# A two-layer transformer kernel on one core: other slots for the same work, the output product in two parts, the setup inside the first slots

## The reference, cut to what matters

```python
xn = layernorm(x)                                   # x: [16, 512, 128]
x  = x + attn0(xn) + ffn0(xn)
xn = layernorm(x)
x  = x + attn1(xn) + moe(xn)

attn0: 16 heads of 8; rope; bias within 64 keys; causal softmax;
       elastic = relu(probs + tau[h] / (row + 1)); (elastic @ v) @ Wo.T
ffn0:  fp4(silu(fp4(xn) @ fp4(Wg).T) * (fp4(xn) @ fp4(Wu).T)) @ fp4(Wd).T    # 352 wide, blocks of 16
attn1: rope; q, k = elu(q) + 1, elu(k) + 1; causal linear attention; @ w_out
moe:   4 experts, the best 2 of a softmax, and a shared one; 344 wide
```

## Time and profile before

| | |
|---|---|
| time, median of 3 runs (lowest to highest) | 2467.56 us (2466.31 to 2469.77) |
| the profiled execution's own time | 2475.17 us |
| its span | 2473.3 us |
| mean granted TensorE clock | 0.939 |
| first scores of round 0; of round 1 | 50.0 us; 151.8 us |
| rounds 2 to 14, each | 148.1 to 151.4 us |
| last round's start to the end | 234.3 us |
| busy: PE, DVE, ACT, POOL | 88%, 74%, 51%, 47% |

### The profile page before, as it was taken

One profiled execution on the slowest core, in us unless ns is written; L12 is line 12 of the kernel. 1 busy time (PEld: TensorE's weight loads), 2 busy tenths in 40 slices (PEclk: granted clock), 3 DMA queues, 4 the chain that ended last, 5 costly groups with the idle time before them and its releaser, 6 DMA issues.

```text
span 2473.3 us, 52472 instructions
## 1 busy us (share of the span) xinstructions
PE 2178.1 (88%) x18761; PEld 1395.3 (56%) x18761; DVE 1820.4 (74%) x5695; ACT 1258.1 (51%) x3477; POOL 1155.4 (47%) x1809
## 2 busy tenths in 40 slices
PE   3788989889898898989889898898989989898988
PEld 2454655646465564655646565565655656565555
DVE  5667868678786877878678686877778678786755
ACT  1555555554544545555554545545455554545532
POOL 6574454534545364454534545354454544534320
PEclk8779989989999999989999899998999989999999
DMA  3000000000000000000000000000000000000000
GB/s 112 5 6 1 1 14 2 14 1 10 5 2 14 1 15 1 1 14 2 14 1 10 5 2 14 1 14 1 2 14 2 14 1 1 10 2 10 2 9 5
DMA packets 33542, 22.03 MB, mean 9 GB/s; under 512 B 2443, under 2 KB 32771, under 8 KB 33283
## 3 DMA queue, kind: packets, MB, share of 16 engines
q1 hardware_dynamic: 33283, 18.68, 2.6%
HBM read 14.48 MB, written 4.19 MB: 8 GB/s over the span
## 4 chain that ended last, share of the span: by engine, by line
PE 69%; DVE 17%; issue 7%; POOL 4%; ACT 3%; DVEq 0%; ACTq 0%; POOLq 0%
PE ps L1084 10%; PE ps L1157 9%; PE ps L1164 8%; PE ps L1216 7%; PE ps L1098 5%; PE ps L1074 4%; DVE ring L491 3%; PE ps L1053 3%; PE ps L1201 3%; PE ps L1150 3%; PE ps L1191 2%; PE ps L1143 2%; PE ps L1062 2%; PE ps L1180 2%; PE ps L1151 2%
## 5 line engine op out<-in xcount | busy, mean ns | idle before, releaser
L801 POOL TENSOR_SCALAR ring<-ring,row_rcp,tau_row 128x128 f32<-128x128 f32 (+3 forms) x1024 | 621.3, 613 | 920.9 <-DVE row_rcp L498 920.6
L903 ACT ACTIVATE ring<-ring,neg_max 128x128 f32<-128x128 f32 (+3 forms) x1024 | 569.1, 556 | 528.8 <-DVE neg_max L491 528.8
L1084 PE MATMUL ps<-identf,ring 128*128 128x128 f32 x2560 | 405.9, 298 | 14.9 <-ACT qkT L894 5.8
L491 DVE CUSTOM_DVE_ANT_1 ring<-ps,bias_t 128x384 f32<-128x384 f32 (+1 forms) x496 | 288.9, 618 | 159.1 <-PE ps L1074 157.0
L1084 PEld LDWEIGHTS ps<-identf,ring 128*128 128x128 f32 x2560 | 295.2, 149 | 86.7 <-issue 23.0
L1216 PEld LDWEIGHTS ps<-ed_t,h 128*128 128x128 f32 (+1 forms) x1920 | 250.6, 191 | 80.6 <-issue 77.6
L1157 PE MATMUL ps<-xn1T,eg_t 128*128 128x512 f32 (+1 forms) x480 | 275.2, 656 | 9.8 <-DVE h L567 9.5
L491 DVE CUSTOM_DVE_ANT_0 ring<-ps,bias_t 128x128 f32<-128x128 f32 (+1 forms) x528 | 170.7, 359 | 139.5 <-PE ps L1074 139.2
L1216 PE MATMUL ps<-ed_t,h 128*128 128x128 f32 (+1 forms) x1920 | 272.7, 278 | 0.0
L1164 PE MATMUL ps<-xn1T,eu_t 128*128 128x512 f32 (+1 forms) x480 | 258.4, 620 | 8.3 <-DVE h L576 5.8
L937 ACT ACTIVATE tanh<-ps 128x512 f32<-128x512 f32 (+1 forms) x240 | 141.3, 589 | 235.9 <-PE ps L1157 235.6
(11 more groups left out here) (154 smaller groups left out, 3378.3 us busy)
## 6 DMA issues: line engine op xcount, KB each, us to landing
x_t<-x SPq DMA_DIRECT2D x16, 256.0 KB, 2.8
x<-x SPq DMA_DIRECT2D x16, 256.0 KB, 2.9
out<-x SPq DMA_DIRECT2D x16, 256.0 KB, 2.3
bias_t<-bias SPq DMA_DIRECT2D x1, 1536.0 KB
eg_t<-eg SPq DMA_DIRECT2D x1, 860.0 KB
eu_t<-eu SPq DMA_DIRECT2D x1, 860.0 KB
ed_t<-ed SPq DMA_DIRECT2D x2, 320.0 KB
ring<-inv_row SPq DMA_DIRECT2D x1, 256.0 KB, 2.6
```

What stands on the lines that cost most here:

```text
L491: dve.tensor_tensor_reduce(out=dst, in0=src, in1=add, scale=-1.0, scalar=NO_MIN, op0=ALU.add, op1=ALU.min, accum_out=neg_max[:, n % 2, r:r ...
L801: pool.tensor_scalar(e, e, row_rcp[:, m % 2, r:r + 1], tau_row[:, i, HG * g + r:HG * g + r + 1], ALU.mult, ALU.add).then_inc(p_ok.sem, 1)
L903: act.activation(e, e, ACT.Exp, bias=neg_max[:, n % 2, r:r + 1], scale=-1.0, accum_out=row_sum[:, n % 2, r:r + 1]).then_inc(exp_ok.sem, 1)
L1084: last = pe.transpose(o[:, r * P:(r + 1) * P], ring_of(i, r)[:, k * P:(k + 1) * P], idf)
```

## The change

The order of the work changes; of the arithmetic, only the order of the summands of the output product and the engines that do the FP4 of the weights. Places by slot (p before, then after):

- gate and up products of layer 0: 14, 15, 16, 17; now 12, 14, 16, 18. Maxima follow by 2, the step moves from 24 to 21, rounding constants from 46-52 to 54-60, add and subtract to 56-63, the last multiply from 56-62 to 64-70, thus into the next round.
- stacks of layer 0: 21, 37, 53, 69; now 27, 45, 59, 73. Future terms: v 77 to 121, y 79 to 123.
- output product: slots 10 to 13; now 6, 8, 9, 11 without the last head group, whose four products stand in slot 12. Only the very first product into bank Y carries the start flag.
- KV 27, 27, 29 to 29, 29, 31; the turn of q from 33 to 29 with a wait of its own for `elu_ok`; LIN, INTRA, TOT and the turn of the linear output later by 0 to 8 slots (TOT 51, 51, 53, 53 to 55, 57, 59, 61; the turn 55 to 63). Experts begin at 25 and keep their last place, 60.
- setup: x is loaded first, then identity, qkv weights and tables, then the FP4 weights. The FP4 of the weights runs on DVE alone in slots 4 to 7 of round -1; PE turns and ACT stores them at slot 12, in other banks. DVE zeroes half of what POOL did. The constants have a semaphore for the attention (round 0) and one for layer 1 (round 1).

```diff
-TURN_X, FUTURE_X, QKV0, TURN_XQ, GATE0 = 5, 7, 7, 11, 14
-STACK0 = (21, 37, 53, 69)
-TURN_H, FUTURE_V, FUTURE_Y = (ATT + 11, ATT + 13, ATT + 13, ATT + 15), ATT + 13, ATT + 15
-WO, ADD_X1 = L1 + 10, L1 + 14
+TURN_X, FUTURE_X, QKV0, TURN_XQ = 5, 7, 7, 11
+GATE0 = (12, 14, 16, 18)
+STACK0 = (27, 45, 59, 73)
+HID_AMAX, HID_STEP, HID_SCALED = [p + 2 for p in GATE0], 21, (38, 39, 40, 41)
+HID_MAGIC, HID_ADD, HID_SUB, HID_MUL = (54, 56, 58, 60), (56, 58, 60, 62), (57, 59, 61, 63), (64, 66, 68, 70)
+TURN_H, FUTURE_V, FUTURE_Y = (ATT + 11, ATT + 13, ATT + 13, ATT + 15), ATT + 57, ATT + 59
+WO, WO_LAST, ADD_X1 = (L1 + 6, L1 + 8, L1 + 9, L1 + 11), L1 + 12, L1 + 14
 TURN_X1, QKV1 = L1 + 19, L1 + 20
-KV, TURN_Q32 = (L1 + 27, L1 + 27, L1 + 29), L1 + 33
-STACK1 = (L1 + 31, L1 + 35, L1 + 39, L1 + 43)
-LIN = [L1 + 33 + v // 2 * 2 for v in range(H)]
-INTRA = (L1 + 37, L1 + 41, L1 + 45, L1 + 49)
-TOT, TURN_O1 = (L1 + 51, L1 + 51, L1 + 53, L1 + 53), L1 + 55
-HID_AMAX, HID_STEP, HID_SCALED, HID_MAGIC, HID_ADD, HID_SUB, HID_MUL = GATE0 + 2, 24, 38, 46, 48, 49, 56
+KV, TURN_Q32 = (L1 + 29, L1 + 29, L1 + 31), L1 + 29
+STACK1 = (L1 + 31, L1 + 35, L1 + 41, L1 + 47)
+LIN = [L1 + (33, 35, 39, 41, 43, 45, 49, 51)[v // 2] for v in range(H)]
+INTRA = (L1 + 37, L1 + 42, L1 + 46, L1 + 53)
+TOT, TURN_O1 = (L1 + 55, L1 + 57, L1 + 59, L1 + 61), L1 + 63
 ROUTER = L1 + 30
-GATE1 = [L1 + 27 + 12 * u // 5 for u in range(3 * NE)]
+GATE1 = [L1 + 25 + 5 * u // 2 for u in range(3 * NE)]
 DOWN1 = [GATE1[3 * e + 2] + 4 for e in range(NE)]
...
-        first = [(identf[:, :], ident)]
...
+        fp4_weights = []
...
+        consts_late = [(bias_t[:, 1:1 + H, 64:256], bias), (wo_t[:, :], wo), (wo_pad_t[:, :, :], wo_pad)]
...
+        N_FIRST, N_WLOAD, N_CONST, N_LATE, N_L1 = (16 * len(v) for v in (first, fp4_weights, consts, consts_late, consts_layer1))
...
+            load(0)
             for dst, src in first:
...
+            for dst, src in fp4_weights:
+                sp.dma_start(dst, src).then_inc(s_wload.sem, 16)
...
                 sp.dma_start(dst, src).then_inc(s_const.sem, 16)
...
                 sp.dma_start(dst, src).then_inc(s_late.sem, 16)
+            for dst, src in consts_layer1:
+                sp.dma_start(dst, src).then_inc(s_l1.sem, 16)
...
+            dve.memset(vx0[:, :, :, :], 0.0).then_inc(s_set.sem, 1)
+            dve.memset(eps_t[:, :], EPS)
+            dve.memset(minus_half[:, :], -0.5).then_inc(s_set.sem, 1)
+            dve.memset(qx[0][:, :, :, :], 0.0)
+            dve.memset(kx[0][:, :, :, :], 0.0)
...
+            dve.memset(bias_t[:, 0, :], 0.0).then_inc(s_set.sem, 1)
+            W, WM = hid[:, 0:BW * FP4], ring[:, L:L + BW * FP4]
...
+            def weights(s):
...
+                if s == 0:
+                    dve.wait_ge(s_first.sem, N_FIRST)
+                    dve.tensor_copy(ident16[:, :], identf[:, :]).then_inc(s_set.sem, 1)
+                if s == 4:
+                    dve.wait_ge(s_wload.sem, N_WLOAD)
+                    dve.wait_ge(s_set.sem, 3)
+                    fp4_steps(W, q_step, BW, s_wq, 0)
+                    dve.wait_ge(s_wq.sem, 3)
+                    dve.tensor_tensor(blocks(W), blocks(W), by_block(q_step[:, 0, 0:BW]), ALU.mult).then_inc(s_wq.sem, 1)
+                if s == 6:
+                    dve.wait_ge(s_wq.sem, 4)
+                    fp4_magic(WM, W, s_wq, 4)
+                    dve.wait_ge(s_wq.sem, 6)
+                    dve.tensor_tensor(W, W, WM, ALU.add).then_inc(s_wq.sem, 1)
+                if s == 7:
+                    dve.wait_ge(s_wq.sem, 7)
+                    dve.tensor_tensor(W, W, WM, ALU.subtract).then_inc(s_wq.sem, 1)
+                    dve.wait_ge(s_wq.sem, 8)
+                    dve.tensor_tensor(blocks(W), blocks(W), by_block(q_step[:, 1, 0:BW]), ALU.mult).then_inc(s_wq.sem, 1)
+                if s == 19:
+                    dve.wait_ge(s_const.sem, N_CONST)
...
+                    dve.tensor_scalar(tau_future[:, :], inv_row_t, tau_col[:, 0:1], 0.0, ALU.mult, ALU.max)
+                    dve.tensor_tensor(tau_row[:, :, :], inv_col_t[:, :].unsqueeze(2).broadcast_to([P, T, H]),
+                                      tau_t[:, :].unsqueeze(1).broadcast_to([P, T, H]), ALU.mult).then_inc(s_set.sem, 1)
...
             pool.memset(vx1[:, :, :], 0.0).then_inc(s_setp.sem, 1)
+            pool.memset(qx[1][:, :, :, :], 0.0)
+            pool.memset(kx[1][:, :, :, :], 0.0)
             pool.wait_ge(s_setp.sem, 1)
...
+            ones = vx1[:, :, 0:H * NV].rearrange("p t (h c) -> p t h c", c=NV)[:, :, :, HD]
...
+            pool.wait_ge(s_set.sem, 2)
...
+                if f == -1 and s == 10:
+                    pool.memset(ones, 1.0).then_inc(s_setp.sem, 1)
+                if f == 0 and s == 0:
+                    pool.wait_ge(s_set.sem, 5)
...
+            act.wait_ge(s_set.sem, 3)
+            def store_weights():
+                for k in range(3):
+                    act.wait_ge(s_wT.sem, k + 1)
...
+                if f == -1 and s == GATE0[0]:
+                    store_weights()
+                if f == 1 and s == 0:
+                    act.wait_ge(s_setp.sem, 2)
...
+            pe.wait_ge(s_set.sem, 4)
...
+            def turn_weights():
+                pe.wait_ge(s_wq.sem, 9)
+                for k in range(2):
+                    for c in range(3):
+                        last = pe.transpose(bank(WEIGHT_BANKS[k])[:, c * P:(c + 1) * P], hid[:, (3 * k + c) * D:(3 * k + c + 1) * D], idf)
...
-            pe.wait_ge(s_wTs.sem, 4)
-            pe.wait_ge(s_const.sem, N_CONST)
-            pe.wait_ge(s_set.sem, 4)
-            pe.wait_ge(s_setp.sem, 4)
...
-                    pe.matmul(bank(Y)[:, t * D:(t + 1) * D], hqT[0:n, t, c, :], wdq[0:n, c, :], start=(c == 0), stop=False)
+                    pe.matmul(bank(Y)[:, t * D:(t + 1) * D], hqT[0:n, t, c, :], wdq[0:n, c, :], start=(t == 0 and c == 0), stop=False)
...
             def attention_out(b, t):
...
                 if t == 0:
-                    pe.wait_ge(os_ok.sem, os_ok.at(b, G))
+                    pe.wait_ge(os_ok.sem, os_ok.at(b, G - 1))
                     pe.wait_ge(s_taken.sem, plan.score["fy", b, 0] + 1)
                 ts = slice(t * P, (t + 1) * P)
                 o = bank(Y)[:, t * D:(t + 1) * D]
                 if t < T - 1:
                     pe.matmul(o, tau_future[:, ts], y_future[:, t, :], start=False, stop=False)
...
+                for g in range(G - 1):
+                    pe.matmul(o, o_stack[:, g, ts], wo_pad_t[:, g, :], start=False, stop=False)
...
+            def attention_out_last(b):
+                pe.wait_ge(os_ok.sem, os_ok.at(b, G))
+                for t in range(T):
+                    last = pe.matmul(bank(Y)[:, t * D:(t + 1) * D], o_stack[:, G - 1, t * P:(t + 1) * P], wo_pad_t[:, G - 1, :],
+                                     start=False, stop=(t == T - 1))
+                last.then_inc(y_ps.sem, 1)
...
-                if 0 <= p - WO < T:
...
+                if p in WO:
+                    down0(b, WO.index(p))
+                    attention_out(b, WO.index(p))
+                if p == WO_LAST:
+                    attention_out_last(b)
...
+                    pe.wait_ge(elu_ok.sem, elu_ok.at(b, T))
...
+                    turn_weights()
+                    pe.wait_ge(s_wTs.sem, 4)
                 if f == 0 and s == 0:
                     pe.wait_ge(s_late.sem, N_LATE)
+                    pe.wait_ge(s_set.sem, 5)
+                if f == 1 and s == 0:
+                    pe.wait_ge(s_l1.sem, N_L1)
+                    pe.wait_ge(s_setp.sem, 2)
```

150 lines of the change are left out of this document (59 added, 91 removed).

## The result

The changed kernel takes 2458.31 us (median of 8 runs, 2453.34 to 2465.07) against 2469.4 us (8 runs, 2466.31 to 2481.4) of the kernel before on the same chip: a ratio of 0.9945, with a 95% interval of 0.9926 to 0.9963. It is faster, by 11 us, where I forecast 95. Its profiled execution has a span of 2463.3 us and a granted clock of 0.955 (before 2473.3 and 0.939).

What follows compares the result with a forecast made beforehand. PE was taken as the limit, a tenth of it idle. Rounds 1 to 14 gave 80 us, start and round 0 13, drain 2: 95 off 2475.2 gives 2380, predicted as 2373 for the median; range 2312 to 2440.

Steps and rivals of the forecast that it cites:

- four terms: Stretches of one round: slots 0-11 27.6, 12-19 16.7, 20-29 20.2, 30-63 77.6 us, sum 142.1; 0.9 added, 143.0.
- KV wait: PE's 3.62 us wait ahead of the KV product for DVE's row maximum, 53.7 us over the span, would get cover.
- slots 20-29: Third stretch of a round: bound by DVE, 20.2 us (ends 19.5 and 21.5), against 21.5 before.
- slots 0-11: First stretch of a round: takes in 2.46 us of output products, 25.1 to 27.6 us (ends 25.1 and 28.6).
- the fourth term: Slots 30-63: bound by PE; 78.3 less 1.3 moved forward plus 0.6 for future terms, 77.6 us.
- slower rival: Slots 55-63: scores wait for TOT's borrowed bank, four waits of 2.2 us; 3.1 us more a round, 2495 us; 9%.
- the second term of the sum: Slots 12-19: 23.8 to 16.7 us, 13.2 of work at full clock and 3.5 idle in four small waits.
- the worth of the clock: In the rounds: PE's lower clock costs little while it waits; some 9 us less at 1.2 GHz for 1 us.
- The start: Setup ahead of the rounds: first gate product 6.3 us earlier, 9 us together (ends 3 and 12).
- The row that I had against the start: At the start, a DVE product stood still until POOL was done; first rope up to 3 us later.
- the signs: Gate waits under half of 61.9 us, KV wait gone, clock 0.97 or more, rounds 141.5 to 144.5 us.
- two signs of being wrong: Among those named: new scores waits for L542 or L521 in slots 55-63; rounds over 146 us.

Runs made afterwards that it cites:

- groups back: Changed kernel with STACK1, LIN, INTRA, TOT, the linear output's turn and the future terms at their slots of before: 2480.56 us, ratio 1.0041.
- old slots: Changed kernel with all slot numbers of both layers put back, keeping the new setup and the output product's split last group: 2469.11 us, ratio 0.9993.
- second half old: norm behind with all slot numbers bearing on slots 30-63 as in the kernel before, except the future terms: 2393.50 us, ratio 0.9686.
- norm behind: Changed kernel with DVE making the gate tile's products ahead of the second layer's statistics and norm in slots 15 and 17: 2431.99 us, ratio 0.9846.
- norm behind and the filler: norm behind plus 12 idle transposes on PE ahead of the last gate tile: 2431.22 us, ratio 0.9835.
- filler: Changed kernel plus 12 transposes that nobody reads, into free bank Y ahead of the last gate tile at slot 18: 2434.86 us, ratio 0.9849.
- gate tiles back: norm behind with the second layer's fifteen gate tiles back in their old slots (27 + 12u/5): 2418.82 us, ratio 0.9787.

## Why the prediction was wrong

In means of rounds 3 to 13 the four terms came out at 27.5, 19.5, 19.5 and 82.4 us for my 27.6, 16.7, 20.2 and 77.6: 148.9 for 143.0. The last term missed by 4.8 us, the second by 2.8.

**Right:** the mechanism of the KV wait (53.7 to 3.5 us), with slots 20-29 at 19.5 us (a new wait of 1.47 us for ScalarE's `vx` took a part); slots 0-11; the future terms at 0.6 us (0.65 by groups back, 0.8 by old slots' 74.45 us in 32-63 and second half old's 75.23). The sign is right by luck: the rounds, from which 80 of my 95 us were to come, brought nothing, and the 11 us stand ahead of round 1.

**Wrong, the fourth term, slots 30-63** ("bound by PE, nothing to gain but work", 77.6 us). The idle time grew from 2.7 to 5.4 us. A stretch in which PE is 97% busy has little to gain from a new order, but it has its small idle time to lose, and I gave that no bound above. In 32-63 two thirds of what was lost (5.2 to 3.4 us, from 2.4) go with the gate tiles' old slots, and these I had priced by the one up product that leaves the stretch, and by no wait. My slower rival named TOT's borrowed bank: its waits came, 18.7 us in 15 rounds or 1.25 a round, against the 6.8 from which it would have decided; and groups back shows that without them the time is waited elsewhere. The work was off as well: total less idle time is 75.6 us before and 77.0 after, where my count had it fall by 0.7. By PE's lines the future terms bring 0.9 us of busy time and a KV product, now in slot 31, 0.5; an up product and the turn of q take 1.0 and 0.4 away. The rest is the same scores (4.9 us before, 6.3 after) and LIN products (2.7, 3.2), each taking longer; why was not taken apart.

**Wrong, the second term of the sum, slots 12-19** ("I keep the idle time of this stretch as it was, 3.5 us, now as four small waits, and give PE its full clock"). The idle time was 4.8 us, 3.0 of it in one wait, and the clock did not hold: 19.5 us less 4.8 leaves 14.8 us for work that I had at 13.2. I had seen that statistics and norm stand ahead of the tile products, and priced them by DVE's load instead of following the chain: the norm has to wait for POOL's root, which stands behind a multiply of probabilities, and the tile's products behind it in DVE's queue. With the norm behind and the filler the stretch took 16.2 us, of which 1.65 idle and 1.47 the filler: 13.1 us of work, as I had counted.

**Wrong, the worth of the clock** ("while PE waits for others, its clock costs little"). The filler shows the price of one fall: about 1.6 us in its place, wherever that is (slots 16-19 of after at 11.24 instead of the filler's 9.68, slots 4-7 of second half old at 10.9 instead of 9.24, slots 0-3 of the filler's own rounds at 9.24 or 7.61). How much of it reaches the round depends on what comes next: all of it at slot 18 of after, half at slots 0-3, where slots 4-7 then take 8.06 us instead of 8.88, a third where DVE sets the next slots. The Trainium skill (TensorE: Matmul & The Clock Gate, HAM oscillation — how this bites in real kernels) has the array put back to half rate by the waits of each pass of a loop. The runs agree for the wait of 2.99 us, behind which the granted clock fell in each of rounds 3 to 14 of after (0.75 to 0.85 in slots 16-19) and stayed at 1.00 in all of them with the filler; it is the weight of this that I had set too low.

**The start:** the setup was given 9 us and brought 1.8 at the first scores of round 1 and nothing in the total. The first gate product came at 30.15 us, just outside my 26 to 30 and 4.2 us earlier than before (forecast 6.3), but the first scores only 3.1: they wait for the stack's transposes and DVE's copy. Batch 0's norm came at 7.91 us (forecast 10.4), but the FP4 of the weights took DVE 11.4 us (forecast 8.5), and the first rope 22.58 (forecast 21). The row that I had against the start points the right way: the second half of the rounding constant (L425, one operand of 1120 columns) took 1.68 us beside POOL's rounding of xq, and 0.74 in before, ahead of POOL's start. Of the four wide products that I had at 1.3 us each, the two without POOL beside them took 1.32, and the two beside it 2.26 and 2.06, though with other operands. Round 0 gave 8.6 us where I had 4.

**Of the signs** I had named, the KV wait went and no other in slots 20-29 is over 1.5 us; the waits of the gate products for DVE grew instead of halving, slots 30-63 are 4.8 us off, and two signs of being wrong came, the scores' wait for TOT's bank and rounds over 146 us.

**Open:** why the gate tiles at 25 + 5u/2 make PE wait more than at 27 + 12u/5. What goes with them is on record: against norm behind, gate tiles back has the scores' waits for `xq` at 6.2 us over the span instead of 19.7 and those for the row maximum at 11.1 instead of 30.6, and LIN's product no longer waits; the order that does it was not taken apart further. Open too is why groups back alone is slower than after (2480.6) while it costs nothing with the norm behind; of the 1.0 us a round, 0.65 stand in slots 0-11 and 0.85 in 12-19 (0.6 of it the future terms), against 0.7 gained in 32-63.

## What to carry to other kernels

Where an engine is 97% busy, ask of a new order what it can lose there, not only what it can gain elsewhere: put the slots of the full stretch back first, and keep only the moves in the stretch that has the idle time. Follow the chain of a wait across all engines up to the instruction that releases it, and issue what the bound engine waits for ahead of what is needed a few slots later. A wait of 1.5 to 3 us ahead of dense products cost here, beside itself, some 1.6 us by the clock when the clock fell; idle products that keep the engine at work through a part of it, into a bank that is free without a wait of its own, brought that second part back. What such a step gives in its place is not what the round keeps: read the next stretches too.

## What the runs showed of the hardware

More instructions on PE made the kernel faster: 12 transposes that nobody reads (1.47 us) gave 1.5 us a round, because the products behind them ran at the granted clock of 1.00. The same eight transposes took 1.09 us at a granted clock of 1.00 and 1.92 at 0.53. The clock fell behind waits of 1.0 to 3.0 us, and behind a wait of the same 1.61 or 1.62 us it fell in some rounds and held in others (slots 4-7 of second half old), so that rounds of one kernel differ by up to 3.5 us (142.2 to 145.7).

DVE took longer for the same instruction beside POOL in two places. The norm of four row tiles took 1.11 us with POOL idle or nearly so, and 1.79 beside its multiplies (before and after). An operation with one operand of 1120 columns took 0.74 us alone (start of before) and 1.68 beside POOL's sums (start of after).
